# State sums by accumulating transposes, a second buffer, and the gate part as its own stream, in a decoder kernel on one core

## The reference, cut to what matters

```
xz = xn @ W_in; xh, z = split(xz)             # 512 + 512 channels
xc = silu(conv(xh)); xpj = xc @ W_xp          # B (16), C (16), dt (1) per token
dt = softplus(xpj[-1:] @ W_dt + b_dt)
h_t = exp(dt * A) * h_(t-1) + dt * B * xc     # 512 channels x 16 states
y_t = sum over the 16 states of h_t * C
out = (y + xc * D) * silu(z) @ W_out + x
```

## Time and profile before

| | |
|---|---|
| median of 3 runs | 1320.05 us (1315.18 to 1323.99) |
| profiled execution, first to last instruction | 1318.1 us |
| PE busy | 1170.0 us (89%), 6026 matmul records |
| PE weight loads busy | 905.1 us (69%) |
| DVE busy | 1038.5 us (79%) |
| ACT busy | 792.2 us (60%) |
| POOL busy | 199.2 us (15%) |
| mean granted clock of PE | 0.953 of full speed |

### The profile page before, as it was taken

One profiled execution on the slowest core, in us unless ns is written; L12 is line 12 of the kernel. 1 busy time (PEld: TensorE's weight loads), 2 busy tenths in 40 slices (PEclk: granted clock), 3 DMA queues, 4 the chain that ended last, 5 costly groups with the idle time before them and its releaser, 6 DMA issues.

```text
span 1318.1 us, 16965 instructions
## 1 busy us (share of the span) xinstructions
PE 1170.0 (89%) x6026; PEld 905.1 (69%) x6026; DVE 1038.5 (79%) x1642; ACT 792.2 (60%) x1978; POOL 199.2 (15%) x258
## 2 busy tenths in 40 slices
PE   5786778988988999999998999999999899999984
PEld 3554545766867767877787777877776767677763
DVE  3999799899878997999869998897959994434215
ACT  4334545378637874686657864875577545646624
POOL 0100020111322212121212121111111211010002
PEclk7888879989999999999999999999999989999998
DMA  5611010223231343233322333322232311000211
GB/s 212 205 44 47 34 54 19 72 63 79 37 96 33 84 86 100 53 65 64 81 72 61 66 56 96 82 51 41 63 87 65 80 33 45 1 1 9 64 63 64
DMA packets 41190, 86.67 MB, mean 66 GB/s; under 512 B 3737, under 2 KB 14970, under 8 KB 40466
## 3 DMA queue, kind: packets, MB, share of 16 engines
q1 hardware_dynamic: 27282, 60.42, 14.4%
q0 software_dynamic: 13824, 25.17, 11.0%
HBM read 54.38 MB, written 6.04 MB: 46 GB/s over the span
## 4 chain that ended last, share of the span: by engine, by line
PE 55%; DVE 25%; ACT 10%; issue 5%; DMA 2%; POOL 2%; ACTq 0%; DVEq 0%; SPq 0%; POOLq 0%
PE bank L295 18%; DVE scans L555 7%; PE bank L510 5%; PE bank L1194 5%; PE bank L1174 4%; DVE scans L560 4%; DVE scans L551 3%; PE bank L906 3%; PE bank L1225 3%; PE bank L900 3%; PE bank L712 3%; ACT scans L531 2%; PE bank L1183 2%; DMA scans<-scans 2%; DVE conv L433 2%
## 5 line engine op out<-in xcount | busy, mean ns | idle before, releaser
L555 DVE TENSOR_TENSOR_SCAN scans<-scans 128x1024 f32<-128x1024 f32 x128 | 292.4, 2284 | 15.3 <-ACT scans L531 8.0
L531 ACT ACTIVATE scans<-dt,a_neg 128x255 f32<-128x255 f32 x512 | 220.7, 502 | 0.0
L510 PE MATMUL bank<-scans,ident 128*128 128x256 f32 x640 | 180.7, 418 | 29.1 <-DVE scans L560 20.2
L510 PEld LDWEIGHTS bank<-scans,ident 128*128 128x128 f32 x640 | 125.0, 206 | 67.2 <-DVE scans L560 26.3
L588 POOL DMA_DIRECT2D scans<-scans x96 | 84.5, 880 | 512.4 <-DVE scans L560 512.2
L560 DVE TENSOR_TENSOR scans<-scans,BC 128x1024 f32<-128x1024 f32 x128 | 155.8, 1217 | 1.3
L551 DVE TENSOR_TENSOR scans<-conv,BC 128x1024 f32<-128x1024 f32 x128 | 155.5, 1215 | 0.1
L1194 PEld LDWEIGHTS bank<-v,ya 128*128 128x128 f32 x1024 | 122.6, 192 | 21.5 <-issue 20.4
L1194 PE MATMUL bank<-v,ya 128*128 128x65 f32 x1024 | 128.5, 276 | 1.8 <-ACT yo L1257 1.6
L1265 ACT ACTIVATE ya<-bank,nmax 128x256 f32<-128x256 f32 x256 | 100.7, 482 | 43.7 <-DVE nmax L1332 43.5
L1332 DVE TENSOR_REDUCE nmax<-bank 128x2 f32<-128x512 f32 x128 | 82.0, 682 | 45.2 <-PE bank L1174 44.8
(11 more groups left out here) (264 smaller groups left out, 2063.8 us busy)
## 6 DMA issues: line engine op xcount, KB each, us to landing
BC<-xpj_scratch SPq DMA_DIRECT2D x31, 1024.0 KB, 5.9
scans<-scans POOLq DMA_DIRECT2D x96, 256.0 KB, 3.3
xin<-in_x SPq DMA_DIRECT2D x8, 256.0 KB, 2.8
conv<-in_x SPq DMA_DIRECT2D x8, 256.0 KB, 2.8
out<-scans SPq DMA_DIRECT2D x8, 256.0 KB, 2.1
kept_x<-x SPq DMA_DIRECT2D x7, 256.0 KB, 2.0
kept_w<-wa SPq DMA_DIRECT2D x7, 256.0 KB, 2.0
BC<-kept_w SPq DMA_DIRECT2D x1, 1792.0 KB, 9.8
```

Of the source, the lines that this page charges most:

```text
L510: last = pe.matmul(sums_of(c), ident[:, :], step_of(b, u)[:, i, :], start=False, stop=(h == UH - 1 and i == SUMMED[b] - 1), skip_group_che ...
L531: ins = act.activation(step[:, j, 1:S], dt[b % 2][:, c, 1:S], ACT.Exp, scale=a_neg[:, c, n:n + 1])
L555: dve.tensor_tensor_scan(flat(H[:, :, :]), flat(H[:, :, :]), flat(dBx), 0.0, ALU.mult, ALU.add).then_inc(s["a_scan"], 1)
```

## The change

1. **Sums by transposes.** The sum over states is no longer a matmul with the identity as stationary operand and 256 columns of state, but for each half of the tokens (`t`) a transpose (`is_transpose=True`, the state as stationary operand, the identity moving) that adds into the bank. y now stands with tokens on the partitions. L501 is turned likewise: xc is stationary, the diagonal matrix moves, 8 matmuls of 128 columns a batch in place of 4 of 256.
2. **Gates turned back.** z is projected with tokens on the partitions (2 products of 512 columns a half). After the gate, PE transposes the gated values back (8 transposes a batch), ACT copies them (2 copies of 128x512), then the product with W_out runs as before. Both gates now follow the last unit.
3. **Second buffer** for `dBx` (`dBx_odd`), and DVE does unit u+1's product with B between unit u's scan and unit u's product with C.
4. **The gate part is a stream G of its own** on SP, PE, ACT, DVE and POOL.
5. **Column norms** of the second layer: PE transposes a broadcast column (2 transposes) in place of 2 ACT operations and a product.
6. **All five order strings are new** (they are not shown). Counted in them: behind the last step of the scan layer PE has 101 steps of Y and 63 of W in the new string, 107 and 62 in the old; DVE 52 of Y and 30 of W, against 55 and 30. In DVE's old string 44 products with B stand directly ahead of their scan and 35 scans directly ahead of their product with C; in the new one a pair that depends on each other stands side by side once. In DVE's new string the next batch's units 0 and 1 stand beside the gate steps of each batch. In PE's, the next batch's L501 stands behind the gate steps.

```diff
--- before.py
+++ after.py
...
-        dBx = scans[:, 3 * HN:4 * HN, :]
+        dBx = [scans[:, 3 * HN:4 * HN, :], sb("dBx_odd", [P, HN, S])[:, :, :]]
 
         def step_of(b, u):
...
                     pe.wait_ge(*of("a_silu_z", b, 1))
-                projected(j, f0)
+                t = j - 2
+                mm(pe, f0[:, :], [(xnT[:, k, t * P:(t + 1) * P], w_in[:, k, DI:]) for k in range(KD)]).then_inc(s["a_in_ps"], 1)
                 yield
...
 
 
-        def sums_of(c):
-            return SA[c // 2][:, (c % 2) * S:(c % 2) * S + S]
-
-
-        SUM_OF = [s["a_sum_0"], s["a_sum_1"], s["a_sum_2"]]
-        ADDED = [NU * b + u for b in range(NB) for u in range(NU) if SUMMED[b] < HN]
+        def sums_of(c, t):
+            return SA[t][:, c * P:(c + 1) * P]
+
+        def gates_of(b, t):
+            return flat(zg[b % 2][:, 2 * t:2 * t + 2, :])
...
                 yield
+
+        def gate_sp(sp, b):
             sp.wait_ge(*of("a_dBx", b))
...
                 pe.wait_ge(s["prep_act"], 6)
-            for c in range(EC):
-                last = pe.matmul(sums_of(c), skips[:, c, :], xc[:, c, :], start=(c % 2 == 0), stop=False, skip_group_check=True)
+            for t in range(T):
+                for c in range(EC):
+                    last = pe.matmul(sums_of(c, t), xc[:, c, t * P:(t + 1) * P], skips[:, c, :], start=(c == 0), stop=False,
+                                     skip_group_check=True)
             last.then_inc(s["a_skip_ps"], 1)
             yield
             for u, (h, c) in enumerate(UNITS):
@@ -507,15 +510,24 @@
                 else:
                     pe.wait_ge(*of_sum(b, u, ADDS[SUMMED[b]]))
                 for i in range(SUMMED[b]):
-                    last = pe.matmul(sums_of(c), ident[:, :], step_of(b, u)[:, i, :], start=False, stop=(h == UH - 1 and i == SUMMED[b] - 1),
-                                     skip_group_check=True)
+                    for t in range(T):
+                        last = pe.matmul(sums_of(c, t), step_of(b, u)[:, i, t * P:(t + 1) * P], ident[:, :], is_transpose=True, start=False,
+                                         stop=(h == UH - 1 and i == SUMMED[b] - 1), skip_group_check=True)
                 last.then_inc(s["a_y_ps"], 1)
                 yield
-            pe.wait_ge(*of("a_gated", b))
+
+        def gate_pe(pe, b):
+            for t in range(T):
+                pe.wait_ge(*of("a_gated", b, t + 1))
+                for c in range(EC):
+                    last = pe.transpose(sums_of(c, t), gates_of(b, t)[:, c * P:(c + 1) * P], ident[:, :])
+                last.then_inc(s["a_out_ps"], 1)
+                yield
             if b == 0:
                 pe.wait_ge(s["loads_first"], N_FIRST)
             for t in range(T):
-                last = mm(pe, SA[t][:, 0:D], [(zg[b % 2][:, c, t * P:(t + 1) * P], w_out[:, c, :]) for c in range(EC)])
+                pe.wait_ge(*of("a_kept", b, t + 1))
+                last = mm(pe, SA[t][:, 0:D], [(gates_of(b, t)[:, c * P:(c + 1) * P], w_out[:, c, :]) for c in range(EC)])
                 last.then_inc(s["a_out_ps"], 1)
                 yield
 
...
                 yield
+
+        def gate_act(act, b):
+            for t in range(T):
+                act.wait_ge(*of("a_out_ps", b, t + 1))
+                act.activation(gates_of(b, t), SA[t][:, :], ACT.Copy).then_inc(s["a_kept"], 1)
+                yield
...
@@ -540,39 +558,44 @@
                 normal(act, conv[b % 2][:, 0:T, :], x1[b % 2], "a1", t).then_inc(s["a1_norm"], 1)
             yield
 
-        def scan_dve(dve, own, b):
-            dve.wait_ge(*of("a_dtx", b))
-            for u, (h, c) in enumerate(UNITS):
-                H, Bh, Ch = step_of(b, u), BC[:, h % 2, 0, :].rearrange("p (n s) -> p n s", n=HN), BC[:, h % 2, 1, :]
+        def scan_dve(dve, b):
+            def weighed_input(u):
+                h, c = UNITS[u]
                 if u == 0 and b == 0:
                     dve.wait_ge(s["prep_act"], 4)
                 elif c == 0:
                     dve.wait_ge(*loaded(b, h))
-                dve.tensor_tensor(dBx, conv[b % 2][:, c:c + 1, :].to_broadcast([P, HN, S]), Bh, ALU.mult).then_inc(s["a_dBx"], 1)
-                yield
+                Bh = BC[:, h % 2, 0, :].rearrange("p (n s) -> p n s", n=HN)
+                dve.tensor_tensor(dBx[u % 2], conv[b % 2][:, c:c + 1, :].to_broadcast([P, HN, S]), Bh, ALU.mult).then_inc(s["a_dBx"], 1)
+
+            dve.wait_ge(*of("a_dtx", b))
+            weighed_input(0)
+            yield
+            for u, (h, c) in enumerate(UNITS):
+                H, Ch = flat(step_of(b, u)), BC[:, h % 2, 1, :]
                 dve.wait_ge(*of("a_dBx", b, u + 1))
                 dve.wait_ge(*of("a_dA", b, 2 * u + 2))
-                dve.tensor_tensor_scan(flat(H[:, :, :]), flat(H[:, :, :]), flat(dBx), 0.0, ALU.mult, ALU.add).then_inc(s["a_scan"], 1)
-                yield
+                dve.tensor_tensor_scan(H, H, flat(dBx[u % 2]), 0.0, ALU.mult, ALU.add).then_inc(s["a_scan"], 1)
+                yield
+                if u < NU - 1:
+                    weighed_input(u + 1)
+                    yield
                 dve.wait_ge(*of("a_scan", b, u + 1))
                 if u == 0 and b == 0:
                     dve.wait_ge(s["prep_act"], 6)
-                dve.tensor_tensor(flat(H[:, :, :]), flat(H[:, :, :]), Ch, ALU.mult).then_inc(s["a_hC"], 1)
-                yield
-                if u == NU - 2:
-                    dve.wait_ge(*of("a_y_ps", b, NU - 2))
-                    dve.wait_ge(*of("a_silu_z", b))
-                    z = flat(zg[b % 2][:, 0:2, :])
-                    dve.tensor_tensor(z, SA[0][:, :], z, ALU.mult).then_inc(s["a_gated"], 1)
-                    yield
+                dve.tensor_tensor(H, H, Ch, ALU.mult).then_inc(s["a_hC"], 1)
+                yield
+
+        def gate_dve(dve, own, b):
             dve.wait_ge(*of("a_y_ps", b))
-            z = flat(zg[b % 2][:, 2:4, :])
-            dve.tensor_tensor(z, SA[1][:, :], z, ALU.mult).then_inc(s["a_gated"], 1)
-            yield
+            dve.wait_ge(*of("a_silu_z", b))
+            for t in range(T):
+                dve.tensor_tensor(gates_of(b, t), SA[t][:, :], gates_of(b, t), ALU.mult).then_inc(s["a_gated"], 1)
+                yield
             dve.wait_ge(*of("a_again", b))
             res, again = conv[b % 2][:, 0:T, :], conv[b % 2][:, T:2 * T, :]
             for t in range(T):
-                dve.wait_ge(*of("a_out_ps", b, t + 1))
+                dve.wait_ge(*of("a_out_ps", b, T + t + 1))
                 dve.scalar_tensor_tensor(res[:, t, :], again[:, t, :], 2.0, SA[t][:, 0:D], ALU.mult, ALU.add).then_inc(s["a_res"], 1)
...
             yield
-            pe.wait_ge(*of("b_diag", b))
-            mm(pe, w1[:, S:2 * S], [(ones[:, :], b_diag[:, :, :].rearrange("p a b -> p (a b)"))]).then_inc(s["b_row_ps"], 1)
+            pe.wait_ge(*of("b_rn", b, 1))
+            for t in range(T):
+                last = pe.transpose(w1[:, S + t * P:S + (t + 1) * P], rn[:, 2 + t:3 + t].to_broadcast([P, P]), ident[:, :])
+            last.then_inc(s["b_row_ps"], 1)
             yield
...
```

More of the change, by code:

```diff
@@ L52 @@
[L52 to L56, removed]
@@ new lines @@
+        "FSWWYWYSWWFWWYYWYSYWYYWYFSYWYWFSYWYSWYYWYSWYYWYYWYFWYSYWYWWSYYWWYWSYYSYYGGYGYGYWSSYYWFYWWYSYYYWFYYWSYYYFSYYWYY"
+        "WYWYFYYWYSYWWYYYWWYWSYWWFWYWWYWSWWWSYYWYYSFYYYWYSYWFYWYWSYYWYYYWYWSYYSWYWYWWWWYSWSWYYFSYYGGYGGYWYSYWWYWYYYSWYY"
+        "YYYWFSYSYYFYYWYWYYYYWWWWSYYYWWYSWYFWWYSYWYWYYSWWYYWWYYWWYYSSYYYWYFWYSFWYYSWYWYYWSYYWYYWWYWYSWYWYWSWYYWYSYYFSYY"
+        "GGYGYGYYWYSWWWYSYWYWYYSYSYYWYYWYYWYYYWSYYYWWYYWSWYYWYYWWSYWYYWWSWYYWYWWSYWSYYYSYWYFWYWYWYWSYYWSYYWYYSWYWYWYWWS"
+        "WYWYSYWYYSYYGYGGGYYWYYWWYWYYWYWYYYYYYYWYYWYYYWYYYWYYWYWWYYWYYWYWWYWYYWWYYWWYWWWYYYYWWYYYYYWYYYWYYWYYWYWYYWYYYW"
@@ L64 @@
[L64 to L68, removed]
@@ L69 @@
-        "YWYYYYYWYYYYYWWYWWWWWWWWWWWWWWWWWWWWW"
+        "FFFFFFFFFSSSSFFSSSSSSSSFSSFSFSFFSSSFFWFSFSSSSSSSSSSSSSSGFGSSSGWSWSSSWFWSFWFWFWSSSSWFFWSSFWWWFWSWSFSWYSYSSSYSYS"
+        "WYYSYSFYYSYYSYFSSYYYSYSSYSYYYSYYFGSFGYYSYYGFYWYWYSYYFSSYFSWYYWYYYSSYWYYYYWSSWFWYYWYYYWSWSYFWYSYSWYFWYSSWSSWSSW"
+        "FYYWWWWSYWYWSSYWSSYWYWSWSYYSYWYYYWSSYYYYWYSSGSSYGYYYYGFSWYYWSYYFYSFYYSFSYYYWWYWYFYYFYSSWYWYFWYYYWSWYYYWYSYFSWW"
+        "SSYFWYSSSYYYSWSFSWWSYYWWWSWSYYSWYWSYWWYSYWYSSYWSSYYWSYSWSYGYGYYYSWYYGYYWYSSYYWYYSYSYSSYYFYYWSYYWYYSFWYYYYYWFYS"
@@ new lines @@
+        "WYWYSWYYYWFWSWSWSYFWSYYYYFSSFWWFWSSYWYWWSSFWSYSYWWYYSYSWWFYYWSSYYSSWYYWYSYWYYSGYGSYSYWGYWYSFSYWYYFYSYYFSYYYSYS"
+        "YWFYWYYYYSSWYYFWWYYSYFWSFYWYWYYWYFWSSWSWYSSYYSYYWWFSSWYYWWWSSWFYSWYYSWSYSYSWWSYWWYSYSYSWWYYSSFSGGYYYWYGYFWYYWY"
+        "SYYSYYYYYFSSSYYWYYWYWYYFSWYYWYWSSYWYYYWYSWSFYWYYYYSSWFSYSWFYYYYSSWWSWSFYWWYSWSFWYSYWWYSYSYWWSWSYYSWYYYWYSSYWYS"
+        "SYFYGSYGSYYYWYGWYWSSYYYYSYSSYWYWYYYWYYSYYYWSSWYYWYYYSWSYWYYWSYYSWYWWYYSSYSSYWWSSWFYYWWSWSWYSWYWSYSSYWWSYYSYWYY"
```

(17 more changed lines are left out.)

42 lines of the change are left out of this document (19 added, 23 removed).

## The result

The changed kernel takes 1300.5 us (median of 4 runs, 1296.0 to 1302.4) against 1320.4: ratio 0.984 [0.981, 0.988], 20 us. Run again on another occasion it gave 0.981 [0.977, 0.985], 26 us. The forecast was 1268, 52 us. The sign was right, the time lies just inside the range, the gain was half of the forecast one at best.

The account below looks back on a forecast made before the run. DVE and PE were taken as both nearly full until 1093.2 us. Second buffer 9.5, own stream 28, PE's relief 12 and tail 2 sum to 51.5 off 1318.1; with 1.95 for the median, 1268 us, range 1238 to 1302.

Parts of the forecast that it names:

- own stream: Seams between batches: DVE goes on with the next batch's units during the gate, regaining 4 us each, 28 over seven.
- PE's relief: Cheaper sums take 60 us off PE; a third of the 35 us in the six later batches counts: 12 us.
- second buffer: Scan on DVE: 79 dependent neighbour pairs at 0.12 us are spared, 9.5 us; the later product with C costs nothing.
- What the gate part adds: Gate chain grows by a gate product, four transposes and a copy, about 2 us; hidden seven times, once on the end.
- Tail: Behind the last scan product: 2 us less, with ends of 5 less and 3 more.
- A: Seam returns as DVE's wait for step buffers after three units, PE's relief unused: 1296 us; chance 15%.
- the 25 named: Sign: DVE's waits before L555 stay below 25 us; 60 or more would mean the step-buffer rival.
- B: No change: DVE's share stays 944 us and freed time returns as other waits, refills above all: about 1316 us; chance 8%.
- C: Slower by the clock: less PE work lowers PE's granted clock; at 0.86 the time is 1347 us; chance 7%.
- the two signs: Mean PE clock until 1093 us: above 0.93 as forecast, below 0.89 for the clock rival.
- 55 to 65: Sign: PE's busy time falls by 55 to 65 us.
- the signs named: DVE over 94% busy from first to last scan product, which ends near 1043 us; forecast wrong if after 1080.

Follow-up runs that it names:

- experiments 1 and 2: Second buffer in old orders: alone on the kernel before 1.050, with DVE's string mended 1.021; with all the change's code 1.040, that code without the buffer 0.998.
- experiment 4: Changed kernel and its new orders with one buffer, product with C directly behind its scan: ratio 0.980 to the kernel before, in both runs.
- experiment 7: Changed kernel with one buffer; from batch 2 on, a batch's last two units summed by PE alone, no adding DMA: 1276.4 us, ratio 0.966.
- e2b: The change's code in the old orders without the second buffer (transposing sums, turned gates, short column norms): 1321 us, ratio 0.998 to the kernel before.
- experiment 3: Changed kernel with sums as ordinary matmuls in place of transposes: all batches 0.994, batches 0 and 1 only 0.992, against the kernel before.
- e3: Changed kernel with the sums of all batches as ordinary float32 matmuls of 128 columns, 1280 records for 640: ratio 0.994 to the kernel before.

## Why the prediction was wrong

Two terms failed. The idle time was to shrink by 40 us between the first and the last scan product (28 by the own stream, 12 by PE's relief) and shrank by 10.8. What is shown to be missing from the sum is the chain of handovers behind a batch's last unit, worth 19 us. And the second buffer's later product with C was costed at nothing and took back all that the buffer gave.

**The second buffer** ("I cost it at nothing; what covers it is the sum that is half as long"). This step failed. The saving on DVE was real, about 8 us busy. The price was not covered: by experiments 1 and 2, 28 to 66 us in orders not made for it, and in the new ones about as much as was saved (experiment 4). I had compared the 1.2 us with the turnover of the step buffers, where there is slack indeed (DVE waited 10.0 us for refills in all). The place that counts is PE's string, where a late sum holds up every layer. 9.5 forecast, 0 measured, give or take 6.

**The own stream** ("I take 4 of it back, 28 us over seven"). This step failed too, and it is the larger one. The seam's idle time was read rightly and did vanish from between the batches, but DVE's whole idle time fell by 10.8 us only. What I missed is the latency of the last unit: product with C, issue and landing of the adding DMA (7.3 us beside the load), sum. I had named the adding DMA only as part of the description, and "What the gate part adds" counted 2 us for the gate's own chain without it. At the seam it stands on the path of PE and DVE together, for both gate products now and not for one half as before, and without it 19 us come back (experiment 7). 28 forecast; put back on DVE in the new orders it costs 42 to 48 us, added alone in the old ones it costs 38, so it has no size apart from the orders. With one buffer, new orders and own stream together are worth 23 us against e2b (0.980 against 0.998).

**PE's relief.** The sizes of the sums were right: 640 records at 0.11 us; the 64 gate transposes are busy 12.0 us, where I had 7. Worth 12 us forecast, 12 to 17 measured, and that is luck, since the reasoning was wrong: nothing in the six later batches, everything in the first two. My reading "DVE is busy 95.3 of 102.5 us there" was of batch 0 alone; in batch 1 DVE was busy 54.13 of 66 us, and experiment 3 shows it waiting for PE there. Why the later batches take nothing from a relief of PE stays open.

**Tail**: 5.1 us in place of 2.

**Rivals.** A gave the best time (1296), but by another mechanism: DVE did not stop on step buffers (waits before the scan 10.0 us, below the 25 named), it stopped on the gate. B is refuted by the ratio. C: the mean clock did fall, 0.953 to 0.929, and lies at 0.93 up to the last scan product, at the upper of the two signs. PE's busy time fell by 41 us, not 55 to 65: the line of the sums by 74.3 (180.7 to 106.4), but beside the 12.0 of the gate transposes the other lines together took 21 us longer, as they would with more of them at half rate. e3, with a clock of 0.956, is slower, so this did not decide. The Trainium skill ("TensorE: Matmul & The Clock Gate", Part 4) says that transposes don't raise the clock as matmuls do, and the runs agree in direction: the same sums as matmuls bring 0.956. But e3 also has twice the records, so the two are not told apart.

Of the signs named: DVE was to be over 94% busy between the scan products, and was 89.6%; the last one was to end near 1043 us, and ended at 1074.4.
